# The spike gate of the first attention: a sigmoid by a power on GpSimd and a reciprocal on VectorE, in place of a ScalarE tangent

## The chip, the cores and the metric

The kernel runs on one core of a Trainium2 chip. The metric is device time in microseconds (us), the median of several runs. A core has five engines with a queue of instructions each, worked off in order: TensorE (PE, matmuls), VectorE (DVE), ScalarE (ACT, tabulated functions), GpSimd (POOL) and SyncE (SP, which here only issues DMAs). They wait for each other through semaphores.

## The reference

Two layers of the same form run over an input `x` of 4 batches x 1024 tokens x 128 channels:

```python
xn = _layernorm(x)
x  = x + attention0(xn) * silu(spiking_ffn(xn))
xn = _layernorm(x)
x  = x + attention1(xn) * silu(coupling_net(xn))
```

Both attentions have 16 heads of 8 channels. The change touches only the `silu` of the first layer. Its argument is the mean of five spikes:

```python
h = jnp.square(jax.nn.relu(xn @ W_fc.T)); y = h @ W_proj.T
mem_new = BETA * mem + y - reset * THRESHOLD       # 5 steps
spk = spike_fn(mem_new - THRESHOLD)                # 0 or 1
return jnp.sum(spks, axis=0) / NUM_STEPS           # n / 5, n = 0..5
```

So the gate is (n/5) * sigmoid(n/5), where n is a whole number from 0 to 5.

## The kernel before

The program has a prologue (norms, projections, transposes), the first attention, the coupling stage (the second layer's feed-forward net, which overlaps the end of the first layer) and the second attention.

The first attention is one long loop over 256 steps `t`: 4 batches of `PER` = 64 steps. A step takes four heads, one tile of 128 keys and 512 queries. For it PE computes scores (L1199, four matmuls, two "units" of 128x1024), ACT takes the exponential of each unit (L1001, two instructions per step), and PE multiplies the result with the values (L1214) into the accumulator `o_ps`. The queues are written out by hand. Three PSUM slots hold units of scores (`SLOTS` = 3), four buffers hold exponentials (`RING` = 4), and the product runs two steps behind the scores (`LAG` = 2). PE and DVE are written in pairs of steps; a batch has 32 pairs, and "pair r" below is the r-th pair of its batch.

Everything else of layer one is slipped into this loop as "side pieces". In each pair PE does at most one (`side_fills` gives the pair for each: the feed-forward `fc` at 5 to 8 and 14 to 17, `y` at 10 to 13 and 19 to 22, the output projection `mix` of the batch's first half at 27, the next layer's `q`, `k`, `v1`, `norm` of the batch before at 18, 23, 24 and 28 to 31). A piece lands in one PSUM bank, `side`. DVE must empty it (`evacuate`) before PE may start the next piece: `pe.wait_ge(side_in, n)` stands at the start of each, and PE's scores and products are queued behind it. Four times in a batch (`end`, pairs 9, 17, 25 and 1 of the next) DVE also transposes `o_ps` out (L1061), and PE's next product waits for that (`o_free`).

The gate belongs to halves `hf` of 512 tokens, tiles of 128x512. In DVE's queue `spike_op` makes n in `y` by 13 instructions from pair 14 (half 0) and pair 23 (half 1) on, two a pair. Then ACT computes tanh(n/10) into `th` (L1006; in the trace `th` has the name `ext`) at steps 42 and 62, and DVE multiplies (1 + tanh) by n (L1091, `gate`) at pair 22, and for half 1 at pair 1 of the next batch (pair 0 after the last). Since (n/5) * sigmoid(n/5) = (n/10) * (1 + tanh(n/10)), the factor `GATE_SCALE` = 1/10 is multiplied into the output weights. `update` on POOL then multiplies the projected attention by the gate (L1013) and adds it to `x` (L1016). POOL also squares the hidden units (L1027) and the `q` and `k` rows of the next layer (`norm_squares`, L1035). The half-norms (`half_norm_op`, small 128x4 instructions of L256 to L264) and `normed_half` (L839) follow on DVE.

After the last batch, `middle` takes over on every engine. Its DVE part waits for all gates (`gated`) before the last update (L1574, L1577, L1578).

Of the kernel before, what the change touches and what calls it, by code (L numbers as in the profile page):

```python
# [20 lines left out]
ALU = mybir.AluOpType  # L21
# [27 lines left out]
BETA = 0.9  # L49
MASK = -1.0e30  # L50
CYCLES = 3
GATE_SCALE = 0.5 / STEPS
ROOT_GUESS = 0x5F3759DF


# [756 lines left out]
def half_norm_tiles(sb):  # L812

    work = {name: sb(name, [P, HT]) for name in ("var", "fix", "root", "rstd")}
    work.update(stats=sb("stats", [P, HT, 6]), moments=sb("moments", [P, HT, 2]))
    return work
# [71 lines left out]
def first_attention(nc, a, s, ctx, room):  # L888
# [38 lines left out]
    th = [s["ext"][1][:, HALF * hf:HALF * hf + HALF].rearrange("p (t c) -> p t c", c=C) for hf in range(2)]  # L927
    square = [early_th1[1][:, HALF * hf:HALF * hf + HALF].bitcast(BF16).rearrange("p (z t) -> p z t", z=2) for hf in range(2)]
    work = half_norm_tiles(sb)

    scores, o_ps, side = room["scores"], room["o_ps"], room["side"]
    side_tiles = side[:, :].rearrange("p (t c) -> p t c", c=C)
# [4 lines left out]
    side_ps, side_in, hid_rdy = sem("side_ps"), sem("side_in"), sem("hid_rdy")  # L937
    xs0_rdy, skip_rdy, spiked, th_rdy, gated = (sem(x) for x in ("xs0_rdy", "skip_rdy", "spiked", "th_rdy", "gated"))
    scaled, updated, ln1, xs1_rdy, scaled_w = (sem(x) for x in ("scaled", "updated", "ln1", "xs1_rdy", "scaled_w"))
    sq_rdy = sem("sq_rdy")  # L940
    stored = [s[f"stored1{hf}"] for hf in range(2)]

    def tiles(b, hf):
        return slice(BT * b + HT * hf, BT * b + HT * hf + HT)
# [48 lines left out]
    def act_part(act):  # L993
        for t in range(S):
            b, gp, qh, gs, kt = place(t)
            if t >= RING:
                act.wait_ge(pv_done, t - RING + 1)
            for pair in range(2):
                unit = 2 * t + pair
                act.wait_ge(scored, unit + 1)  # L1000
                nc.scalar.activation(probs[t % RING][:, 2 * pair:2 * pair + 2, :], scores[unit % SLOTS][:, :, :],  # L1001
                                     ACT.Exp).then_inc(expd, 1)
            for hf, at in ((0, 42), (1, 62)):
                if t % PER == at:
                    act.wait_ge(spiked, SPIKE_OPS * (2 * b + hf + 1))
                    nc.scalar.activation(th[hf][:, :, :], s["y"][:, tiles(b, hf), :], ACT.Tanh,  # L1006
                                         scale=GATE_SCALE).then_inc(th_rdy, 1)

    def pool_part(pool):
        def update(b, hf):  # L1010
            pool.wait_ge(side_in, fill_index("mix", b, hf) + 1)
            pool.wait_ge(gated, 2 * b + hf + 1)
            pool.tensor_tensor(mix[hf][:, :, :], mix[hf][:, :, :], s["y"][:, tiles(b, hf), :], ALU.mult).then_inc(scaled, 1)  # L1013
            pool.wait_ge(scaled, 2 * b + hf + 1)
            x = s["x"][:, tiles(b, hf), :]
            pool.tensor_tensor(x, x, mix[hf][:, :, :], ALU.add).then_inc(updated, 1)  # L1016

        def skips(b):
            for hf in range(2):
                pool.wait_ge(xs0_rdy, 2 * b + hf + 1)  # L1020
                skip = s["xn"][:, tiles(b, hf), :]
                pool.tensor_tensor(skip, skip, s["bo"][:, 0:1, :].broadcast_to([P, HT, C]), ALU.add).then_inc(skip_rdy, 1)

        def squares(b, hf):
            for f in range(FC):
                pool.wait_ge(side_in, fill_index("fc", b, (hf, f)) + 1)
                pool.tensor_tensor(hidden[f], hidden[f], hidden[f], ALU.mult).then_inc(hid_rdy, 1)  # L1027

        def norm_squares(b, hf):
            for z in range(2):  # L1030
                pool.wait_ge(side_in, fill_index("qk"[z], b, hf) + 1)
                if b > 0:
                    pool.wait_ge(side_in, fill_index("norm", b - 1, hf) + 1)
                high = parts[hf][:, z, 0, :].bitcast(F32)
                pool.tensor_tensor(square[hf][:, z, :], high, high, ALU.mult).then_inc(sq_rdy, 1)  # L1035

        for b in range(B):
            if b > 0:
                update(b - 1, 1)
                skips(b)  # L1040
            squares(b, 0)
            if b == 0:
                pool.wait_ge(scaled_w, 1)
                skips(b)
            squares(b, 1)
            if b > 0:
                norm_squares(b - 1, 0)
            update(b, 0)
            if b > 0:
                norm_squares(b - 1, 1)  # L1050

    def dve_part(dve):
        ends, spike, norm1 = Chain(dve, end_link), Chain(dve, spiked), Chain(dve, ln1)

        def end(e):
            t = turn[e % 2]
# [31 lines left out]
        def gate(b, hf):  # L1088
            y = s["y"][:, tiles(b, hf), :]
            dve.wait_ge(th_rdy, 2 * b + hf + 1)  # L1090
            nc.vector.scalar_tensor_tensor(y, th[hf][:, :, :], 1.0, y, ALU.add, ALU.mult).then_inc(gated, 1)  # L1091

        def extra(b, r):
            if b == 0 and r == 9:
# [3 lines left out]
            if b == 0 and r == 13:  # L1098
# [2 lines left out]
                nc.vector.tensor_scalar_mul(s["bo"][:, 1, :], s["bo"][:, 1, :], 0.5)  # L1101
                nc.vector.tensor_scalar_mul(s["w1"][:, 0, :], s["w1"][:, 0, :], SCALE)
                nc.vector.tensor_scalar_mul(s["b_col1"][:, 0:1], s["b_col1"][:, 0:1], SCALE).then_inc(scaled_w, 1)
            if b > 0 and r == (0 if b == B else 1):
                gate(b - 1, 1)
            if b == 1 and r == 3:
                room["constants"](dve)
            if b < B:
# [6 lines left out]
                for k in range(SPIKE_OPS):  # L1115
                    for hf, at in ((0, 14), (1, 23)):
                        if r == at + k // 2:
                            spike_op(b, hf, k)
                if r == 22:
                    gate(b, 0)  # L1120
            for hf, at, own in ((1, 6, b - 1), (0, 29, b)):
                if 0 <= own < B and not (own == B - 1 and hf == 1):
# [1099 lines left out]
```

## Time and profile before

| | |
|---|---|
| median of 3 runs | 897.27 us (896.77 to 897.57) |
| profiled execution, first to last instruction | 894.0 us, so 3.3 us lie outside it, seen against the median |
| first attention (55.9 to 534.6 us) | 478.7 us |
| busy there | ACT 476.8, PE 454.5, DVE 241.0, POOL 84.2 us |
| coupling stage (534.6 to 602) | 67.4 us: PE 60.8, DVE 58.4, ACT 47.0 us |
| second attention (602 to 894) | 292.0 us |

The trace lists each instruction with its start, duration, engine, line, and output and input tiles. In brackets stands the idle time of its engine just before it, and what released it. Two matmul or ScalarE instructions in a row overlap in part, so the step from start to start is the cost of one in a full queue, and it is shorter than the duration. A share of busy time tells little here: what counts is which engine waits, in which pair, for whom.

### The profile page before, as it was taken

Reading aid. Unit: us, or ns where it says so; the run is one execution under the profiler, and the core shown is the slowest. Engines: PE = TensorE matmul, PEld = TensorE weight load, DVE = VectorE, ACT = ScalarE, POOL = GpSimd, SP = SyncE. Lnnn points to the kernel's source line nnn. Section 1 sums busy time; section 2 is a strip of 40 time slices with the busy share of each in tenths; the row PEclk is TensorE's granted clock in tenths of the full one; section 3 lists DMA queues with packets and bytes.
Section 4 is the critical chain, followed back from the end, with each engine's and each line's share of the span. In section 5 each row is a group of like instructions: output and inputs, shape, how many; then the busy total and the mean of one; then the engine's idle time right before and its main releaser. Section 6 shows DMA issues by size and latency. Waiting matters only on the chain.

```text
span 894.0 us, 22254 instructions
## 1 busy us (share of the span) xinstructions
PE 781.4 (87%) x9422; PEld 304.8 (34%) x9422; DVE 398.4 (45%) x862; ACT 832.1 (93%) x929; POOL 217.4 (24%) x260
## 2 busy tenths in 40 slices
PE   4849999899999999998999999978888888887876
PEld 2412434234343433433343333223333332332322
DVE  7821164454647553576327577994211021121122
ACT  7759999999999999999999996778999999999896
POOL 2201120121212041111303023103342443334343
PEclk9969999999999999999999999998999999999999
DMA  7882020110210301203000016000202202112000
GB/s 185 280 289 44 3 76 3 34 44 2 77 49 1 124 2 32 70 25 123 2 3 25 25 58 206 23 25 1 76 3 88 79 11 88 38 52 88 12 3 25
DMA packets 31950, 53.47 MB, mean 60 GB/s; under 512 B 5481, under 2 KB 16361, under 8 KB 31849
## 3 DMA queue, kind: packets, MB, share of 16 engines
q1 hardware_dynamic: 31848, 52.01, 18.7%
q8 instruction: 76, 1.25, 0.6%
q14 instruction: 26, 0.21, 0.1%
HBM read 31.29 MB, written 20.71 MB: 58 GB/s over the span
## 4 chain that ended last, share of the span: by engine, by line
PE 70%; ACT 18%; issue 3%; DVE 3%; ACTq 0%; DVEq 0%
PE c_ps L1214 25%; PE c_ps L1199 13%; ACT c_ring L1883 11%; PE c_ps L2071 10%; PE c_ps L112 10%; PE c_ps L2028 7%; ACT c_ring L1001 5%; PE c_ps L1619 2%; DVE early L1564 1%; PE c_ps L1634 1%; PE c_ps L1626 1%; ACT xs L1890 1%; ACT c_ring L1422 1%; DVE y L1567 1%; ACT ext L1006 0%
## 5 line engine op out<-in xcount | busy, mean ns | idle before, releaser
L1001 ACT ACTIVATE c_ring<-c_ps 128x1024 f32<-128x1024 f32 x512 | 473.7, 1034 | 9.5 <-PE c_ps L1199 9.2
L1883 ACT ACTIVATE c_ring<-c_ps 128x1024 f32<-128x1024 f32 x288 | 269.5, 1049 | 10.5 <-PE c_ps L2028 4.8
L1214 PE MATMUL c_ps<-c_ring,vt 128*18 128x256 f32 (+1 forms) x3072 | 271.3, 456 | 0.0
L1199 PE MATMUL c_ps<-q_st,k_st 32*128 32x512 f32 x1024 | 131.1, 500 | 28.8 <-ACT c_ring L1001 23.3
L2071 PE MATMUL c_ps<-c_ring,vt 128*18 128x256 f32 (+3 forms) x1856 | 154.0, 440 | 0.8
L1908 POOL TENSOR_SCALAR_AFFINE_SELECT c_ring<-c_ring 128x512 f32<-128x512 f32 x128 | 85.8, 690 | 191.7 <-ACT c_ring L1883 191.7
L2028 PE MATMUL c_ps<-q_st,k_st 32*128 32x512 f32 (+3 forms) x768 | 78.2, 422 | 51.3 <-ACT c_ring L1883 50.7
L1214 PEld LDWEIGHTS c_ps<-c_ring,vt 128*18 128x18 f32 x3072 | 65.2, 97 | 143.2 <-issue 103.0
L1199 PEld LDWEIGHTS c_ps<-q_st,k_st 32*128 32x128 f32 x1024 | 50.6, 183 | 144.7 <-ACT c_ring L1001 135.4
L1027 POOL TENSOR_TENSOR early<-early 128x512 f32<-128x512 f32 x32 | 38.4, 1201 | 177.4 <-DVE early L1138 177.4
L2028 PEld LDWEIGHTS c_ps<-q_st,k_st 32*128 32x128 f32 x768 | 36.9, 184 | 113.0 <-ACT c_ring L1883 103.1
L1942 DVE STREAM_TRANSPOSE ext<-c_ps 128x512 f32<-128x512 f32 x15 | 10.8, 717 | 135.5 <-PE c_ps L2071 135.5
L2071 PEld LDWEIGHTS c_ps<-c_ring,vt 128*18 128x18 f32 x1856 | 40.7, 97 | 70.3 <-issue 51.4
L1138 DVE TENSOR_SCALAR early<-c_ps 128x512 f32<-128x512 f32 x32 | 22.1, 690 | 67.2 <-PE c_ps L112 67.2
L1142 DVE TENSOR_SCALAR y<-c_ps,rho 128x128 f32<-128x128 f32 x32 | 9.0, 344 | 92.6 <-PE c_ps L112 92.6
L1013 POOL TENSOR_TENSOR early<-early,y 128x512 f32<-128x512 f32 x7 | 10.6, 1513 | 144.5 <-DVE early L1153 144.5
L1422 ACT ACTIVATE c_ring<-c_ps,cn_b 128x512 f32<-128x512 f32 (+1 forms) x30 | 25.1, 858 | 16.6 <-PE c_ps L1619 11.3
L1035 POOL TENSOR_TENSOR c_th<-parts 128x512 bf16<-128x512 f32 x12 | 15.1, 1256 | 82.7 <-DVE parts L1170 82.7
L112 PE MATMUL c_ps<-proj_t,early 128*32 128x128 f32 x1024 | 33.8, 273 | 0.0
L112 PE MATMUL c_ps<-y,fc_t 128*32 128x512 f32 x256 | 33.3, 592 | 0.0
L112 PEld LDWEIGHTS c_ps<-proj_t,early 128*32 128x32 f32 x1024 | 29.3, 110 | 5.9
L1084 DVE SCALAR_TENSOR_TENSOR c_th<-ext,c_th 128x512 f32<-128x512 f32 x24 | 25.5, 1061 | 0.7
(238 smaller groups left out, 727.4 us busy)
## 6 DMA issues: line engine op xcount, KB each, us to landing
q_st<-q_hl SPq DMA_DIRECT2D x48, 256.0 KB
k_st<-k_hl SPq DMA_DIRECT2D x48, 256.0 KB
q_hl<-parts SPq DMA_DIRECT2D x12, 512.0 KB, 4.4
k_hl<-parts SPq DMA_DIRECT2D x12, 512.0 KB, 4.7
q_hl<-early SPq DMA_DIRECT2D x4, 512.0 KB, 4.8
k_hl<-early SPq DMA_DIRECT2D x4, 512.0 KB, 5.2
out_dram<-x SPq DMA_DIRECT2D x7, 256.0 KB, 4.1
x<-in_L_attn_x_dram SPq DMA_DIRECT2D x3, 512.0 KB, 5.7
```

The costliest lines, as they stand in the source:

```text
L112: ins = nc.tensor.matmul(out[c:c + COLUMN, :], weight[:, c:c + COLUMN], rows, start=start, stop=stop, tile_position=(0, c))
L1001: nc.scalar.activation(probs[t % RING][:, 2 * pair:2 * pair + 2, :], scores[unit % SLOTS][:, :, :], ACT.Exp).then_inc(expd, 1)
L1027: pool.tensor_tensor(hidden[f], hidden[f], hidden[f], ALU.mult).then_inc(hid_rdy, 1)
L1084: ins = nc.vector.scalar_tensor_tensor(y if step == STEPS - 1 else count[:, :, :], m1, 1.0, count[:, :, :], ALU.is_gt, ALU.add)
L1138: ins = nc.vector.tensor_scalar_max(hidden[hf[1]], side[:, :], 0.0)
L1199: ins = nc.tensor.matmul(scores[(2 * t + i // 2) % SLOTS][:, i % 2, :], k_st[part, g, kt * P:(kt + 1) * P], q_st[part, g, qh * HALF:(qh + ...
L1214: ins = nc.tensor.matmul(o_ps[32 * h:32 * h + 2 * W9, c0:c1], vt[b % 2][:, kt, gp, h, W9 * gs:W9 * gs + 2 * W9], probs[t % RING][:, h, c0: ...
L1422: nc.scalar.activation(out, source, ACT.Gelu, bias=bias[:, 0:1]).then_inc(squashed[z], 1)
L1883: nc.scalar.activation(probs[t % RING][:, 2 * pair:2 * pair + 2, :], scores[unit % SLOTS][:, :, :], ACT.Exp).then_inc(expd, 1)
L1908: ins = pool.affine_select(out=part, in_=part, compare_op=ALU.is_ge, fill=0.0, base=0, pattern=[[0, G], [1, P]], channel_multiplier=-1)
L2028: ins = nc.tensor.matmul(banks[i][:, at:at + w], k_st[part, 2 * gp + gs, kt * P:(kt + 1) * P], q_st[part, 2 * gp + gs, qh * HALF + q0:qh * ...
L2071: ins = nc.tensor.matmul(o_ps[32 * h:32 * h + 2 * W9, q0:q0 + w], vt[b % 2][:, kt, gp, h, W9 * gs:W9 * gs + 2 * W9], probs[t % RING][:, h, ...
```

## The change

The gate's sigmoid becomes 1 / (1 + exp(-n/5)). The power `DECAY ** n` = exp(-n/5) is one POOL instruction per half (`powers`), with the constant base broadcast from a new tile `decay`. DVE's `gate` now has three dependent instructions: add 1, reciprocal, and the product with n. `GATE_SCALE` becomes 1/5. ACT's eight tangents are gone. In POOL's queue the power of half 0 comes behind the two squares of `norm_squares(b - 1, 0)`, that of half 1 behind `norm_squares(b - 1, 1)`. The gates stand later in DVE's queue: at pair 27 in place of 22, at pair 3 in place of 1, and after the last batch at pair 1 in place of 0, which puts it behind the last `end`.

```diff
-GATE_SCALE = 0.5 / STEPS
+GATE_SCALE = 1.0 / STEPS
+DECAY = float(np.exp(-GATE_SCALE))
...
-            for hf, at in ((0, 42), (1, 62)):
-                if t % PER == at:
-                    act.wait_ge(spiked, SPIKE_OPS * (2 * b + hf + 1))
-                    nc.scalar.activation(th[hf][:, :, :], s["y"][:, tiles(b, hf), :], ACT.Tanh,
-                                         scale=GATE_SCALE).then_inc(th_rdy, 1)
...
+        def powers(b, hf):
+            pool.wait_ge(spiked, SPIKE_OPS * (2 * b + hf + 1))
+            pool.tensor_tensor(th[hf][:, :, :], decay[:, :, 0:1].broadcast_to([P, HT, C]), s["y"][:, tiles(b, hf), :],
+                               ALU.pow).then_inc(th_rdy, 1)
...
+        pool.memset(decay[:, :, :], DECAY).then_inc(decay_rdy, 1)
+        pool.wait_ge(decay_rdy, 1)
...
             if b > 0:
                 norm_squares(b - 1, 0)
+            powers(b, 0)
             update(b, 0)
             if b > 0:
                 norm_squares(b - 1, 1)
+            powers(b, 1)
...
-            nc.vector.scalar_tensor_tensor(y, th[hf][:, :, :], 1.0, y, ALU.add, ALU.mult).then_inc(gated, 1)
+            below.after(nc.vector.tensor_scalar(th[hf][:, :, :], th[hf][:, :, :], 1.0, None, ALU.add))
+            below.after(nc.vector.reciprocal(th[hf][:, :, :], th[hf][:, :, :]))
+            nc.vector.tensor_tensor(y, y, th[hf][:, :, :], ALU.mult).then_inc(gated, 1)
...
-            if b > 0 and r == (0 if b == B else 1):
+            if b > 0 and r == (1 if b == B else 3):
                 gate(b - 1, 1)
...
-                if r == 22:
+                if r == 27:
                     gate(b, 0)
```

How the queues stand afterwards. First DVE in the last batch, around pairs 22 to 29. Of the program before: L1142 is the `y` evacuation at pair 22, L1091 the gate, L1153 the `mix` evacuation at pair 27, L1174 the `norm` evacuation at pair 28, L1169 and L1170 that of `q` at 29.

```order
L1142 TENSOR_SCALAR y<-c_ps,rho 128x128 x4
L1091 SCALAR_TENSOR_TENSOR y<-ext,y 128x512
L1169 TENSOR_SCALAR parts<-c_ps,b_col 128x512
L1170 SCALAR_TENSOR_TENSOR parts<-c_ps,b_col,parts 128x512
...
L1153 TENSOR_TENSOR early<-c_ps,xn 128x512
L1082 SCALAR_TENSOR_TENSOR ext<-ext 128x512
L1084 SCALAR_TENSOR_TENSOR c_th<-ext,c_th 128x512
L1174 TENSOR_REDUCE norms<-c_ps 64x1
```

The same stretch of the changed program, where these lines are L1151, L1178, L1179, L1162, L1089, L1091 and L1183:

```order
L1151 TENSOR_SCALAR y<-c_ps,rho 128x128 x4
L1178 TENSOR_SCALAR parts<-c_ps,b_col 128x512
L1179 SCALAR_TENSOR_TENSOR parts<-c_ps,b_col,parts 128x512
...
L1162 TENSOR_TENSOR early<-c_ps,xn 128x512
L1089 SCALAR_TENSOR_TENSOR ext<-ext 128x512
L1091 SCALAR_TENSOR_TENSOR c_th<-ext,c_th 128x512
L1098 TENSOR_SCALAR ext<-ext 128x512
L1099 RECIPROCAL ext<-ext 128x512
L1100 TENSOR_TENSOR y<-y,ext 128x512
L1183 TENSOR_REDUCE norms<-c_ps 64x1
```

The gate, now three instructions, moved from the front of this stretch to a place directly ahead of the `norm` evacuation.

Then POOL in the last batch, from the squares of the hidden units to the coupling stage (L1406, squares of the last half). Before:

```order
L1027 TENSOR_TENSOR early<-early 128x512 x8
L1035 TENSOR_TENSOR c_th<-parts 128x512 x2
L1013 TENSOR_TENSOR early<-early,y 128x512
L1016 TENSOR_TENSOR x<-x,early 128x512
L1035 TENSOR_TENSOR c_th<-parts 128x512 x2
L1406 TENSOR_TENSOR ext<-parts 128x512 x2
```

And in the changed program, where L1025 are the hidden squares, L1038 the row squares, L1029 the power, L1011 and L1014 the update:

```order
L1025 TENSOR_TENSOR early<-early 128x512 x8
L1038 TENSOR_TENSOR c_th<-parts 128x512 x2
L1029 TENSOR_TENSOR ext<-a_decay,y 128x512
L1011 TENSOR_TENSOR early<-early,y 128x512
L1014 TENSOR_TENSOR x<-x,early 128x512
L1038 TENSOR_TENSOR c_th<-parts 128x512 x2
L1029 TENSOR_TENSOR ext<-a_decay,y 128x512
L1415 TENSOR_TENSOR ext<-parts 128x512 x2
```

Each power stands behind a pair of row squares; the first is ahead of the update, the second ahead of whatever POOL does next.

## Rows read from the trace of the kernel before

**Rows 1.** Groups by line: line engine op tiles xcount | busy us, mean ns | idle before.
```profile
L1001 ACT ACTIVATE c_ring<-c_ps 128x1024 f32<-128x1024 f32 x512 | 473.7, 1034 | 9.5 <-PE c_ps L1199 9.2 <-issue 0.2
L1199 PE MATMUL c_ps<-q_st,k_st 32*128 32x512 f32 x1024 | 131.1, 500 | 28.8 <-ACT c_ring L1001 23.3 <-DVE c_ps L1177 4.6
L1006 ACT ACTIVATE ext<-y 128x512 f32<-128x512 f32 x8 | 5.1, 637 | 0.0
```

**Rows 2.** Busy time by engine (PE, PEld, DVE, ACT, POOL) in the first attention.
```profile
55.90:534.60 478.70, 454.54 (x6096) 176.13 (x6096) 241.04 (x514) 476.83 (x520) 84.22 (x66) 0.99 0.15 46
```

**Rows 3.** Timeline, ACT: start us, us, engine line op tiles xcount [idle before].
```profile
137.28 0.63 ACT L1006 ACTIVATE ext<-y 128x512 f32<-128x512 f32 x1
137.79 36.88 ACT L1001 ACTIVATE c_ring<-c_ps 128x1024 f32<-128x1024 f32 x40
```

**Rows 4.** Timeline, PE weight loads, last batch: waits for ACT in one pair.
```profile
502.12 0.19 PEld L1199 LDWEIGHTS c_ps<-q_st,k_st 32*128 32x128 f32 x4 [0.84 <-ACT c_ring L1001]
505.84 0.19 PEld L1199 LDWEIGHTS c_ps<-q_st,k_st 32*128 32x128 f32 x4 [0.20 <-ACT c_ring L1001]
506.73 0.12 PEld L1214 LDWEIGHTS c_ps<-c_ring,vt 128*18 128x18 f32 x4 [0.31 <-ACT c_ring L1001]
```

**Rows 5.** Timeline, POOL and DVE side by side, 119 to 126 us.
```profile
119.14 1.42 POOL L1027 TENSOR_TENSOR early<-early 128x512 f32<-128x512 f32 x1 [2.29 <-DVE early L1138]
119.70 1.41 DVE L1082 SCALAR_TENSOR_TENSOR ext<-ext 128x512 f32<-128x512 f32 x1
...
125.46 0.69 DVE L1082 SCALAR_TENSOR_TENSOR ext<-ext 128x512 f32<-128x512 f32 x1
```

**Rows 6.** Timeline, POOL and DVE side by side, 530 us.
```profile
530.02 1.04 POOL L1035 TENSOR_TENSOR c_th<-parts 128x512 bf16<-128x512 f32 x1 [2.67 <-DVE parts L1170]
...
530.04 1.03 DVE L264 SCALAR_TENSOR_TENSOR a_root<-a_fix,a_root 128x4 f32<-128x4 f32 x1
```

**Rows 7.** Groups by line and form, DVE: reciprocals of three sizes, and an add-like scalar instruction.
```profile
L138 DVE RECIPROCAL a_recip<-early 128x32 f32<-128x32 f32 x16 | 5.6, 353 | 0.5
L138 DVE RECIPROCAL a_recip<-ext 128x16 f32<-128x16 f32 x2 | 0.5, 252 | 0.1
L1078 DVE TENSOR_SCALAR c_th<-y 128x512 f32<-128x512 f32 x8 | 3.3, 417 | 0.0
```

**Rows 8.** Timeline, POOL: products of 128x512 with one and with two input tiles.
```profile
78.42 1.04 POOL L1027 TENSOR_TENSOR early<-early 128x512 f32<-128x512 f32 x1 [39.73 <-DVE early L1138]
193.75 1.31 POOL L1013 TENSOR_TENSOR early<-early,y 128x512 f32<-128x512 f32 x1 [30.23 <-DVE early L1153]
```

**Rows 9.** Timeline, last batch, pairs 24 and 25: POOL, DVE and PE.
```profile
503.88 1.15 POOL L1035 TENSOR_TENSOR c_th<-parts 128x512 bf16<-128x512 f32 x1 [17.55 <-DVE parts L1170]
504.17 1.41 DVE L1080 SCALAR_TENSOR_TENSOR ext<-y 128x512 f32<-128x512 f32 x1
...
506.59 0.68 DVE L1082 SCALAR_TENSOR_TENSOR ext<-y,ext 128x512 f32<-128x512 f32 x1
...
508.83 0.72 DVE L1061 STREAM_TRANSPOSE early<-c_ps 128x512 f32<-128x512 f32 x1 [0.83 <-PE c_ps L1214]
...
509.90 1.49 PE L1214 MATMUL c_ps<-c_ring,vt 128*18 128x512 f32 x16
```

**Rows 10.** Timeline, DVE, last batch, pairs 27 to 29.
```profile
516.99 0.69 DVE L1153 TENSOR_TENSOR early<-c_ps,xn 128x512 f32<-128x512 f32 x1 [1.78 <-PE c_ps L112]
...
524.31 0.75 DVE L1169 TENSOR_SCALAR parts<-c_ps,b_col 128x512 fp32r<-128x512 f32 x1 [1.93 <-PE c_ps L112]
```

**Rows 11.** Timeline, last batch, pair 31 and after: DVE and PE weight loads.
```profile
531.11 0.16 DVE L261 SCALAR_TENSOR_TENSOR a_fix<-a_root 128x4 f32<-128x4 f32 x1
...
532.18 0.68 DVE L1172 TENSOR_TENSOR xn<-c_ps,bv 128x512 f32<-128x512 f32 x1
...
533.55 0.10 PEld L1249 LDWEIGHTS c_ps<-c_th,head_of 128*32 128x32 bf16 x2
```

**Rows 12.** Timeline, DVE, start of the coupling stage.
```profile
539.61 0.69 DVE L1574 TENSOR_TENSOR early<-c_ps,xn 128x512 f32<-128x512 f32 x1 [1.11 <-PE c_ps L1688]
...
552.36 0.68 DVE L1541 TENSOR_REDUCE norms<-c_ps 64x1 f32<-64x512 f32 x1 [2.56 <-PE c_ps L1675]
```

**Rows 13.** Timeline, DVE, batch 0 after half 0's spikes, and batch 1's first pairs.
```profile
140.97 1.13 DVE L1142 TENSOR_SCALAR y<-c_ps,rho 128x128 f32<-128x128 f32 x4 [11.91 <-PE c_ps L112]
...
181.05 0.72 DVE L1061 STREAM_TRANSPOSE early<-c_ps 128x512 f32<-128x512 f32 x1 [10.80 <-PE c_ps L1214]
```

More of the change, by code:

```diff
@@ L929, in first_attention @@
     work = half_norm_tiles(sb)
+    decay = sb("decay", [P, HT, 1])
     scores, o_ps, side = room["scores"], room["o_ps"], room["side"]
@@ L939, in first_attention @@
     scaled, updated, ln1, xs1_rdy, scaled_w = (sem(x) for x in ("scaled", "updated", "ln1", "xs1_rdy", "scaled_w"))
-    sq_rdy = sem("sq_rdy")
+    sq_rdy, decay_rdy = sem("sq_rdy"), sem("decay_rdy")
+    denominator = sem("denominator")
     stored = [s[f"stored1{hf}"] for hf in range(2)]
@@ L1050, in pool_part @@
                 norm_squares(b - 1, 1)
+            powers(b, 1)
     def dve_part(dve):
-        ends, spike, norm1 = Chain(dve, end_link), Chain(dve, spiked), Chain(dve, ln1)
+        ends, spike, norm1, below = (Chain(dve, x) for x in (end_link, spiked, ln1, denominator))
         def end(e):
```

## The prediction

> **What bounds the kernel now.** I read the groups by line first, then the busy time by stage, then the timeline of each engine around the gates. In the first attention ACT is busy 476.8 of 478.7 us [rows 2]. Its 512 exponentials waited only 9.5 us in all, nearly all of it before the first [rows 1]. So ACT is full from the loop's start to its end, and a tangent in its queue costs its whole step: 137.28 to 137.79, 0.51 us [rows 3]. But the margins of the others are thin. PE waits for ACT only for 0.20 to 0.84 us ahead of a step's scores, the less the larger the side piece, and 0.31 us within the products [rows 4]. When PE comes later than that, ACT runs dry within a few exponentials. PE in turn waits for DVE wherever `side` or `o_ps` must be emptied. So I asked at each place where the change adds something how late DVE gets, and whether PE notices.
>
> **What is taken away.** Eight tangents at 0.51 to 0.52 us: -4.2 us, if nothing else gives way.
>
> **The reciprocal.** The trace has none of 128x512. Those of L138 take 353 ns for 32 elements a row and 252 ns for 16 [rows 7]: 6.3 ns per element. Carried on to 512 that is 0.353 + 480 x 0.0063 = 3.4 us. With the addition (as L1078, 0.42 us [rows 7]) and the product (0.69 us [rows 5]) the gate holds DVE for 4.5 us; before it was 0.7. Ends: if the slope belonged only to small strided rows, a 128x512 instruction of DVE takes 0.69 us [rows 5], and the gate 1.8; above, I allow 4.5 us for the reciprocal, a third more than the slope. I take 3.4, since both rows are of the very operation.
>
> The Trainium skill (VectorE: DVE Perf Modes, "First, the fixed hardware budget") says that a reciprocal is an iterated divide with a repeat count of 8. At the 0.96 GHz of the same page's specifications that is an estimated 4.3 us for 512 elements; the rows show 6 rather than 8 such cycles per element, and they decide. By the page the forecast would be some 3 us higher.
>
> **The power.** No row shows one. From below, it does at least what a POOL product of two tiles does, 1.31 us [rows 8]. From above I build it out of passes: a logarithm, a product and an exponential, each function a polynomial of several terms, make at most some 20 operations; each costs no more than a whole product pass of 1.04 us [rows 8], 21 us together. The ends are a factor 16 apart, and no row is near. I take their geometric mean, 5.2 us (five product passes), and call it X. The duration is not the whole cost, because of the following.
>
> **What a POOL instruction does to DVE.** L1082 takes 0.69 us alone. It took 1.41 us when it started at 119.70 inside the POOL product of 119.14 to 120.56, and ended 0.55 us behind it: it made no progress in between [rows 5]. A DVE instruction of 128x4, too, took 1.03 us and ended with the POOL instruction beside it [rows 6]. So DVE instructions with two SBUF inputs stand still while POOL works on SBUF. If that holds for the power, everything in DVE's queue waits up to X.
>
> For products of 1 us the rows show this; that a long, computing instruction holds the port to its end they don't. The Trainium skill (SBUF — State Buffer, "Who interferes with whom") has it so: the pair of ports is an exclusive lock that the first instruction keeps to its end. By that rule the sum is the one below; if the port were free while the power computes, it would be about 4 us.
>
> **Place A, the power of half 0** (batches 1 to 3). It is behind the second row square, which ends at 505.03; the DVE instruction already waiting goes first and ends at 505.58 [rows 9]. So the power runs 505.6 to 510.8. L1082, due at 506.59, and the spike instruction behind it then end at 512.2, and the `o_ps` transpose at 512.95 in place of 509.55. PE's first product of the next step, which started at 509.90 [rows 9], waits for it: 3.05 us late, of which 0.3 are PE's slack [rows 4]. Stall 2.8 us, three times: 8.3. In batch 0 no row squares stand ahead; the power starts with DVE's 11.9 us of idle time [rows 13] and is free.
>
> **Place B, the gate at pair 27** (batches 1 to 3). From L1153 to the `q` evacuation DVE has 1.93 us of idle time [rows 10]. The gate brings 4.5. The `norm` evacuation behind it and then `q` and `k` are late by 2.6 us; less 0.5 of PE's slack (the middle of 0.20 to 0.84 [rows 4]) that is 2.1, three times: 6.3. In addition the POOL update starts about 5.7 us later and blocks DVE among the following evacuations rather than before: DVE's and POOL's queues go into pair 31 about 1.8 us behind ACT (0.5 of the slack used, 1.3 for one POOL instruction).
>
> **Place C, the power of half 1** (batches 1 and 2). It starts behind the last row square, 531.1, and holds DVE's small root instructions until 536.3; six of them (531.11 to 532.18) and L1172 (0.68) follow [rows 11], so `v1` is emptied at 538.05 in place of 532.86. PE's `norm` piece, which began at 533.55 [rows 11], waits: 4.5 us, with the lag 6.3. Up to two and a half exponentials of 0.92 us (36.88/40 [rows 3]) are in stock, 2.3 us. Stall 4.0, twice: 8.0. After batch 0 DVE is idle for 10.8 us [rows 13]: free. The gate at pair 3 there falls into idle time.
>
> **The end.** In the last batch nothing covers place C: PE's last products, the last `end` and the coupling stage's PE queue all come 6.3 us later. The gate now stands behind that `end`, so L1574, which had 1.11 us to spare, is 3.4 us late against PE; 2.56 us of idle time at 552.36 [rows 12] take most of that back. I put down 0.5 (between 0 and 0.9). The second attention is unchanged.
>
> **Sum.** -4.2 + 8.3 + 6.3 + 8.0 + 6.3 + 0.5 = +25.2 us. The profiled span is 894.0, so 919.2; with the 3.3 us by which the median of the runs lies above it, 922.5.
>
> With X the sum moves by 6 us per us (three places A, two C, the end), once X is over some 3.5. Below, A is free up to 2.4 and C up to 1.2. X = 3.5 gives +15, X = 8 gives +42, X = 10 gives +54, X = 12 gives +66, X = 21 gives +120.
>
> **Rivals.**
> 1. *The power is cheap, or leaves DVE's port alone.* With X = 1.31: -4.2, A 0, B 6.3, C 0.2, end 1.31 + 1.1 = 2.4, and 0.5: +5.2, 902.5. With a free port and X under 8 about the same (+4, 901). For it: no row shows a computing instruction hold the port. Against: the power is no single arithmetic step.
> 2. *A long power*, 8.5 us and more: +45 to +120, 942 to 1017. For it: a general power with its special cases may be longer than five passes. Against: only my way of counting.
> 3. *Faster: the reciprocal streams.* At 0.69 us the gate is 1.8 us, less than the 1.93 of idle time at B, so B costs nothing and no lag is left. With X = 1.31 the end costs some 1.5 us: -4.2 + 1.5 + 0.3 = -2.4, 894.9. It decides at X = 2.3 with such a reciprocal, and with one of 2 us only if X is under 1.5. Against it stand the two sizes of [rows 7].
> 4. *Nothing to be measured*: these cancel by chance, X about 2.3 with a short reciprocal.
> That ACT isn't relieved at all I rule out: the tangents are gone from its queue, and none is left to load or run.
>
> **How the numbers follow.** Forecast (port held, X 3.5 to 8.5): 0.42, with its own range of 910 to 943. Rival 1: 0.26 (X up to 3.5 with the port held, to 912, included). Rival 2: 0.20. Rival 3: 0.07. Rival 4: 0.05. The range leaves out rival 3, rival 4 in part, and powers over 12 us (about 0.1): 899 to 964. A difference of under 0.2% (1.8 us) can't be told from none here: faster 0.08, same 0.05, slower 0.87.
>
> **What would show it.** POOL's rows of the power give X; the row of the 128x512 reciprocal should read 3.4 us. With the port held, a DVE instruction behind each power has a duration of nearly X, and ACT has idle gaps that it doesn't have now: about 2.8 us at pair 25, some three of together 2 at pairs 28 to 30, 4 us at pair 0 of the next batch, none in batch 0. If the port is free, DVE's rows beside the power keep 0.69 us. The forecast is wrong if ACT shows no gaps at pairs 28 to 30 though the reciprocal takes over 3 us, or if the coupling stage takes up or gives back more than 1 us.

## The result, and the profile after

The changed kernel takes 1438.08 us (median of 4 runs, 1436.89 to 1438.62) against 897.02 us for the kernel before: 1.6038 times as long, 95% interval 1.6016 to 1.606. The forecast of 922.5 us, and its range up to 964, were far too low. The direction was right, the reason only in part.

The groups by line of the kernel after (columns as in [rows 1]) name the place at once.

```profile
L1004 ACT ACTIVATE c_ring<-c_ps 128x1024 f32<-128x1024 f32 x512 | 474.7, 1032 | 476.8 <-PE c_ps L1208 476.2
L1029 POOL TENSOR_TENSOR ext<-a_decay,y 128x512 f32<-128x512 f32 x8 | 656.8, 82097 | 4.9 <-DVE y L1091 4.9
...
L1098 DVE TENSOR_SCALAR ext<-ext 128x512 f32<-128x512 f32 x8 | 4.2, 531 | 539.8 <-POOL ext L1029 539.8
...
L1099 DVE RECIPROCAL ext<-ext 128x512 f32<-128x512 f32 x8 | 26.8, 3353 | 0.3
```

One power (L1029) takes 82.1 us. DVE's addition (L1098), the first instruction of each gate, waits 539.8 us for it in all. The exponentials (L1004) do the same work as before, 474.7 against 473.7 us, but stand idle for 476.8 us instead of 9.5 [rows 1]. The reciprocal takes 3.35 us.

The slices of the page (busy tenths in 40 slices, 36 us each) show the same as a picture.

```profile
PE   5699804039910801993061099405007888888887
...
DVE  8314213044500502451060135305008911121112
ACT  7699913029920800993062099503005799999997
POOL 2015989961499798139979822997992133333333
PEclk9799956569965855997576599757658999999999
```

POOL is full through most of the first attention (up to slice 28) while ACT, which was full in [rows 2], works in bursts. Where PE is at 0, the clock falls too.

How one engine's wait stops the others is read from ACT's timeline (start us, us, instructions, idle time before them), one line per power. The first:

```profile
177.73 5.67 ACT L1004 ACTIVATE c_ring<-c_ps 128x1024 f32<-128x1024 f32 x6
228.60 3.95 ACT L1004 ACTIVATE c_ring<-c_ps 128x1024 f32<-128x1024 f32 x4 [45.21 <-PE c_ps L1208]
```

The next two, and one that is no longer in the first attention:

```profile
312.41 1.94 ACT L1004 ACTIVATE c_ring<-c_ps 128x1024 f32<-128x1024 f32 x2 [70.67 <-PE c_ps L1208]
...
1083.78 0.26 ACT L1474 ACTIVATE n_gu<-c_ps,cn_gb 64x2 f32<-64x2 f32 x1 [73.41 <-PE c_ps L1669]
```

Five more gaps lie between the last two: 70.44 us before 472.62, 731.09 and 988.52, 66.7 us before 570.20 and 828.79. The seven gaps up to 988.52 are 460.6 us together; the eighth is in the coupling stage. What ACT is said to wait for is PE; what PE waits for stands in the list of waits (engine, line, for what: us in total, times, longest).

```profile
DVE ext L1098 <- POOL ext L1029: 539.8, 8, 74.8
...
PE c_ps L113 <- DVE norms L1183: 207.6, 3, 69.2
...
PE c_ps L113 <- DVE early L1162: 200.3, 3, 69.4
...
PE c_ps L1669 <- DVE n_mean L1560: 74.4, 1, 74.4
...
PE c_ps L1223 <- issue: 43.7, 1, 43.7
```

So the chain is power, addition, everything queued behind it on DVE (`norms`, `early`, `n_mean`), PE's next piece of work, and with it the scores that ACT needs. Behind six of the powers PE stands at a side piece whose bank DVE has not emptied. Behind the eighth it waits for the norm of the coupling stage. The first gap goes another way: no side piece is due there, and the trace names no releaser for PE's product at 225.01 ("issue"). It starts 0.1 us after DVE's transpose of `o_ps` has ended, for which that product waits in the program (`o_free`):

```profile
224.20 0.71 DVE L1068 STREAM_TRANSPOSE early<-c_ps 128x512 f32<-128x512 f32 x1
```

The account of the profiled execution, 1436.3 against 894.0 us, +542.3. The first attention ends with ACT's table load at 998.95, before at 534.62: +464.3. Of that +467.3 are idle time before L1004 (476.8 - 9.5), +1.0 its busy time, and -4.2 the eight tangents as forecast: +464.1. The coupling stage runs from there to the next table load, 141.5 us against 64.4: +77.1, of which 73.4 is the eighth gap. The remaining 0.9 us lies behind it.

### The profile page after: what moved, and what is told of

Read it like the earlier page. It is cut to its first block, busy times and chain, and to the rows that moved or that the text cites. A ratio compares the mean times of both kernels' runs of the same rounds, so it can differ in the third digit from the quotient of the medians.

```text
span 1436.3 us, 22272 instructions
## 1 busy us (share of the span) xinstructions
PE 799.6 (56%) x9422; PEld 306.6 (21%) x9422; DVE 433.1 (30%) x878; ACT 830.4 (58%) x921; POOL 872.3 (61%) x269
## 4 chain that ended last, share of the span: by engine, by line
POOL 46%; PE 33%; ACT 8%; DVE 7%; issue 2%; ACTq 0%; DVEq 0%
POOL ext L1029 46%; PE c_ps L1223 10%; PE c_ps L2080 6%; ACT c_ring L1892 6%; PE c_ps L113 5%; PE c_ps L1208 5%; PE c_ps L2037 5%; DVE ext L1099 2%; PE c_ps L1628 1%; DVE early L1573 1%; ACT c_ring L1004 1%; POOL c_th L1038 0%; PE c_ps L1643 0%; DVE ext L1087 0%; DVE parts L1179 0%
## 5 line engine op out<-in xcount | busy, mean ns | idle before, releaser
L1004 ACT ACTIVATE c_ring<-c_ps 128x1024 f32<-128x1024 f32 x512 | 474.7, 1032 | 476.8 <-PE c_ps L1208 476.2
L1029 POOL TENSOR_TENSOR ext<-a_decay,y 128x512 f32<-128x512 f32 x8 | 656.8, 82097 | 4.9 <-DVE y L1091 4.9
L1223 PE MATMUL c_ps<-c_ring,vt 128*18 128x256 f32 (+1 forms) x3072 | 278.5, 466 | 43.7 <-issue 43.7
L1892 ACT ACTIVATE c_ring<-c_ps 128x1024 f32<-128x1024 f32 x288 | 269.6, 1048 | 11.2 <-PE c_ps L2043 5.2
L1098 DVE TENSOR_SCALAR ext<-ext 128x512 f32<-128x512 f32 x8 | 4.2, 531 | 539.8 <-POOL ext L1029 539.8
L1208 PE MATMUL c_ps<-q_st,k_st 32*128 32x512 f32 x1024 | 133.4, 509 | 27.1 <-ACT c_ring L1004 20.8
L1025 POOL TENSOR_TENSOR early<-early 128x512 f32<-128x512 f32 x32 | 38.4, 1199 | 162.6 <-DVE early L1147 162.6
L113 PE MATMUL c_ps<-y,w 128*32 128x512 f32 x96 | 15.2, 709 | 207.6 <-DVE norms L1183 207.6
L1038 POOL TENSOR_TENSOR c_th<-parts 128x512 bf16<-128x512 f32 x12 | 15.1, 1256 | 73.3 <-DVE parts L1179 73.3
L113 PEld LDWEIGHTS c_ps<-y,fc_t 128*32 128x32 f32 x256 | 8.2, 113 | 207.0 <-DVE early L1162 201.7
L113 PEld LDWEIGHTS c_ps<-y,w 128*32 128x32 f32 x96 | 2.9, 117 | 210.7 <-DVE norms L1183 209.1
```

Of the source, the lines that this page charges most:

```text
L113: ins = nc.tensor.matmul(out[c:c + COLUMN, :], weight[:, c:c + COLUMN], rows, start=start, stop=stop, tile_position=(0, c))
L1029: pool.tensor_tensor(th[hf][:, :, :], decay[:, :, 0:1].broadcast_to([P, HT, C]), s["y"][:, tiles(b, hf), :], ALU.pow).then_inc(th_rdy, 1)
L1208: ins = nc.tensor.matmul(scores[(2 * t + i // 2) % SLOTS][:, i % 2, :], k_st[part, g, kt * P:(kt + 1) * P], q_st[part, g, qh * HALF:(qh + ...
L1223: ins = nc.tensor.matmul(o_ps[32 * h:32 * h + 2 * W9, c0:c1], vt[b % 2][:, kt, gp, h, W9 * gs:W9 * gs + 2 * W9], probs[t % RING][:, h, c0: ...
```

## The experiments

All but the one marked are compared with the kernel before on the same chip. Its median was 896.16 us for the first three, 896.21 for the four from "The product, with half 0's gate at pair 26" on, and 896.43 for the last. A difference in us is the ratio with its interval, applied to that median. Where the power is replaced or cut down, the values are not the reference's; these kernels only price it.

**A product in place of the power.** Everything else of the change stays, so this prices the change with a short POOL instruction: it takes 1.04 to 1.48 us.

```
-                               ALU.pow).then_inc(th_rdy, 1)
+                               ALU.mult).then_inc(th_rdy, 1)
```

> The changed kernel with a POOL product in place of the power, same tiles, same place in the queue (so the gate's value is not the reference's). Theory 1 (the power's own length, 82 us, makes the loss; everything else in my sum is right): the sum at X = 1.31 us stands, -4.2 for the tangents, +6.3 at the gates of pair 27, +2.4 at the end, +0.2 +0.5: +5.2 us, 902; ACT shows idle gaps of together about 2 us at pairs 28 to 30 of batches 1 to 3. Rival (the longer gate is hidden, only the power cost anything): -4.2 + at most 1, so 893 to 894, no ACT gaps.

Measured: 900.91 us, ratio 1.0056 (1.0043 to 1.0068), so +5.0 us. ACT's timeline at pairs 28 to 30 of batch 1:

```profile
287.81 3.79 ACT L1004 ACTIVATE c_ring<-c_ps 128x1024 f32<-128x1024 f32 x4 [0.79 <-PE c_ps L1208]
292.66 3.79 ACT L1004 ACTIVATE c_ring<-c_ps 128x1024 f32<-128x1024 f32 x4 [1.05 <-PE c_ps L1208]
297.03 110.98 ACT L1004 ACTIVATE c_ring<-c_ps 128x1024 f32<-128x1024 f32 x120 [0.58 <-PE c_ps L1208]
```

Three gaps, 2.4 us together; batches 2 and 3 show 2.2 and 2.4. That is place B of the prediction. By the medians, 1438.08 - 900.91, the power's length is worth 537 us of the change's cost, all but five.

The sum agrees better than its terms do. Place B is 7.0 us in place of 6.3. The end, put down at 2.4 + 0.5 us, shows no gap of its own: the coupling stage takes 65.2 us here and 64.6 with the narrow power below, against 64.4 before. (This profiled execution took 903.1 us, 2.2 above the median; it has one more gap, 1.28 us at 70.84, that the narrow power's does not show.)

**The product, and no reciprocal.** The gate loses its reciprocal, which changes the values and leaves 1.1 us of work on DVE.

```
-            below.after(nc.vector.reciprocal(th[hf][:, :, :], th[hf][:, :, :]))
```

> As the product kernel, and the reciprocal left out as well, so that the gate is an addition and a product, 1.1 us of DVE. Theory 1 (place B is DVE's hold of 4.5 us against 1.93 us of idle time): the gaps at pairs 28 to 30 go, the sum is -4.2 plus some 1.5 to 2 at the end: about -2.4, 894.6. Rival (the gate's place at pair 27 costs, not its length): as the product kernel within 1 us.

Measured: 893.44 us, ratio 0.9975 (0.9964 to 0.9986), so -2.2 us. The gaps at pairs 28 to 30 are gone:

```profile
279.03 12.97 ACT L1004 ACTIVATE c_ring<-c_ps 128x1024 f32<-128x1024 f32 x14
292.21 8.36 ACT L1004 ACTIVATE c_ring<-c_ps 128x1024 f32<-128x1024 f32 x9 [0.21 <-issue]
```

The reciprocal alone makes the difference of 7.5 us between this kernel and the product kernel. Rival 3 had the sum for this case, -2.4; here too the terms differ. The loop, from ACT's second group of exponentials to its table load, is 3.2 us shorter than before rather than 4.2, and the coupling stage is 64.6 us, so that of the 1.8 us at the end 0.2 are seen.

**A narrow power.** A power on 32 of each row's 512 elements: long enough to tell whether DVE's port is held, short enough to end before every gate (L1102, the addition, waits 0.0 us in its trace). The other elements hold what a product wrote in batch 0.

```
-            pool.tensor_tensor(th[hf][:, :, :], ..., ALU.pow).then_inc(th_rdy, 1)
+            pool.tensor_tensor(th[hf][:, :, 0:8], ..., ALU.pow).then_inc(th_rdy, 1)
```

(`th[hf]` holds 4 tiles of 128, so 0:8 of each is 32 elements a row. The product of batch 0 stands in lines that are not shown.)

> The changed kernel with the power taken on 32 of each row's 512 elements (8 of 128 columns; the rest of the tile is filled once by a product and then left as it is, so the gate's value is not the reference's). If 82 us is a price per element, 160 ns each, the power now takes 5.1 us, the length that I had forecast. Theory 1 (the power leaves DVE's port free, so that only the wait in the gate costs, and 5.1 us end before the gate is due): +4 us, 901, DVE's instructions beside it at 0.69 us. Rival (port held, as in the forecast): +25 us, 922, with a DVE instruction of up to 5 us behind each power.

Measured: 901.32 us, ratio 1.0065 (1.005 to 1.0079), so +5.8 us, the product kernel's time within the intervals. POOL's power and the DVE instructions beside it, in batch 3 at place A:

```profile
506.19 5.87 POOL L1033 TENSOR_TENSOR ext<-a_decay,y 128x32 f32<-128x32 f32 x1
```

```profile
507.17 0.69 DVE L1185 TENSOR_TENSOR xn<-c_ps,bv 128x512 f32<-128x512 f32 x1 [0.40 <-PE c_ps L113]
507.78 0.68 DVE L1093 SCALAR_TENSOR_TENSOR ext<-y,ext 128x512 f32<-128x512 f32 x1
508.50 0.69 DVE L1095 SCALAR_TENSOR_TENSOR c_th<-ext,c_th 128x512 f32<-128x512 f32 x1
510.01 0.72 DVE L1072 STREAM_TRANSPOSE early<-c_ps 128x512 f32<-128x512 f32 x1 [0.82 <-PE c_ps L1227]
```

This power has almost exactly the X of my forecast (5.6 us on average, 5.2 taken). By the forecast the kernel should have cost +25 us. It does not, because the DVE instruction with two SBUF inputs at 507.78 takes its usual 0.68 us in the middle of the power. So the port is not held through the power: the second assumption of the forecast falls, independently of the power's length.

**The power by itself** (one execution; its total time is not compared). Eight POOL instructions one after the other, appended to the kernel before at the end of its second attention.

```
+ go(pool.tensor_tensor(res[:, 0:128], base[:, 0:128], bent[:, 0:128], ALU.pow))   # 0.81873 ^ 3
+ go(pool.tensor_tensor(res[:, 0:32], ...))  and  0:4,  and 16 partitions
+ go(... five ...)   go(... half ...)   go(... ALU.mult)   go(bent ^ half)
```

> The kernel before with POOL instructions appended to the end of POOL's queue, on tiles that nothing else uses: powers of 128x128, 128x32, 128x4 and 16x128, of 128x128 with exponents 3, 5 and 0.5 and with base 3, and one product of 128x128. Theory 1 (a price per element of a row, whatever the values, partitions side by side): 20.5, 5.1 and 0.7 us for the widths, 20.5 us for 16 partitions too, and the same for every exponent. Rival a (a large fixed part, such as code that is loaded): the narrow ones far above 160 ns per element. Rival b (the price depends on the values): exponents 0.5 and 5 differ from 3 by over 10%. The time of the whole kernel is longer by the appended work and is not compared.

Their rows, in that order, from POOL's timeline:

```profile
893.48 20.80 POOL L1949 TENSOR_TENSOR bench<-bench 128x128 f32<-128x128 f32 x1
914.36 5.43 POOL L1950 TENSOR_TENSOR bench<-bench 128x32 f32<-128x32 f32 x1
919.87 1.01 POOL L1951 TENSOR_TENSOR bench<-bench 128x4 f32<-128x4 f32 x1
920.95 20.77 POOL L1952 TENSOR_TENSOR bench<-bench 16x128 f32<-16x128 f32 x1
941.80 20.78 POOL L1953 TENSOR_TENSOR bench<-bench 128x128 f32<-128x128 f32 x1
962.66 20.77 POOL L1954 TENSOR_TENSOR bench<-bench 128x128 f32<-128x128 f32 x1
983.51 0.45 POOL L1955 TENSOR_TENSOR bench<-bench 128x128 f32<-128x128 f32 x1
984.04 20.77 POOL L1956 TENSOR_TENSOR bench<-bench 128x128 f32<-128x128 f32 x1
```

From 32 to 128 elements a row: (20.80 - 5.43)/96 = 0.160 us per element, and 0.3 us that is fixed. 512 x 0.160 = 82 us, which is what the changed kernel shows. Sixteen partitions cost as much as 128, and exponents 3, 5 and 0.5 and bases 0.82 and 3 cost the same. A product of 128x128 takes 0.45 us, 1/46 of the power. So the price is one of each element of a row, and neither the other values tried nor fewer partitions lower it.

**The product, with half 0's gate at pair 26.** The forecast put place B down to the meeting of the gate with the side pieces of pairs 27 to 29. If so, one pair earlier is enough.

```
-                if r == 27:
+                if r == 26:
```

> The product kernel (a POOL product in place of the power) with the gate of half 0 at pair 26 in place of 27. Pair 26 has no side piece, so more of DVE's idle time lies behind the gate before PE needs the next bank. Theory (place B is a matter of which pair takes DVE's 4.5 us): the gaps of together 2.1 to 2.4 us in batches 1 to 3 shrink to under 0.5, some 5 us less than the product kernel, so 895 to 896, about the time before. Rival (DVE's hold costs the same wherever it stands): as the product kernel, 901.

Measured: 894.21 us, ratio 0.9978 (0.9967 to 0.999), so -2.0 us; 6.7 less than the product kernel. In its timeline ACT goes through pairs 26 to 31 with one gap of 0.20 us. So place B needs both the long gate and this position: either change by itself removes it. What the move would be worth behind an 82-us power was not run.

**The position alone.** The kernel before, tangents and all, with its gates at the changed kernel's places.

```
-            if b > 0 and r == (0 if b == B else 1):
+            if b > 0 and r == (1 if b == B else 3):
...
-                if r == 22:
+                if r == 27:
```

> The kernel before, tangents and one-instruction gate kept, with the gates at pairs 27, 3 and 1 in place of 22, 1 and 0. Theory (0.7 us of DVE at pair 27 fits into 1.93 us of idle time): within 0.5 us of before. Rival (a late gate delays the update of x and with it the squares, norms and the next layer's rows): 1 to 3 us slower.

Measured: 895.48 us, ratio 1.000 (0.9989 to 1.001). A gate of 0.7 us costs nothing in these places.

**A gate without tangent and power, two instructions.** `y` holds spike counts, whole numbers from 0 to 5. On these a quadratic fits the sigmoid to within 4.4 parts in 10,000, so that y times the gate is a cubic; its scale goes into the kernel's existing constant.

```
-                    nc.scalar.activation(th[hf][:, :, :], ..., ACT.Tanh, scale=GATE_SCALE).then_inc(th_rdy, 1)
...
-            nc.vector.scalar_tensor_tensor(y, th[hf][:, :, :], 1.0, y, ALU.add, ALU.mult).then_inc(gated, 1)
+            below.after(nc.vector.scalar_tensor_tensor(th[hf][:, :, :], y, -41.369491771299835, y, ALU.add, ALU.mult))
+            nc.vector.scalar_tensor_tensor(y, th[hf][:, :, :], -388.1519156907403, y, ALU.add, ALU.mult).then_inc(gated, 1)
```

The gates stay at the places of the kernel before, pairs 22, 1 and 0, and not at those of the change.

> The kernel before without tangents and without POOL: n takes only the values 0 to 5, so DVE evaluates the sigmoid as a quadratic in n, the gate as n times it: two instructions with two inputs each, (n + c) * n and then (that + d) * n, at the gate's old places; the factor goes into the output weights. Largest relative error of the gate 4e-4. Theory (ACT is full, a tangent costs its 0.52 us, and 0.7 us more of DVE at pairs 22, 1 and 0 lies in idle time): -4.2 + 0.3 at the last gate, 892 to 892.5. Rival (ACT was not the bound, PE is, the relief is lost): within 1 us of before.

Measured: 894.42 us, ratio 0.9977 (0.9963 to 0.999), so -2.1 us. It is faster than both kernels, by less than expected. In its timeline the exponentials run from 65.51 to the table load at 531.61, 466.1 us; before it was 65.30 to 534.62, 469.3. So 3.2 of the 4.2 us of tangents come out. It has two gaps of 0.2 us, where the kernel before has one; the second is:

```profile
529.65 1.94 ACT L1001 ACTIVATE c_ring<-c_ps 128x1024 f32<-128x1024 f32 x2 [0.21 <-issue]
```

The other 0.8 us is in the pace of the exponentials, which no row puts down to a cause. The kernels without tangents and without gaps at pairs 28 to 30 agree: their loops are 2.8 us (gate at pair 26) and 3.2 us (no reciprocal, two instructions, three instructions) shorter than before. The coupling stage then takes 64.8 us instead of 64.4.

**The same with three instructions.** A fit to within 2.4 parts in 100,000. The other constants change too; the added line is:

```
+            below.after(nc.vector.scalar_tensor_tensor(th[hf][:, :, :], th[hf][:, :, :], -446.7958912964597, y, ALU.add, ALU.mult))
```

> As the cubic gate with one instruction more (a cubic for the sigmoid, largest relative error 2.4e-5), so the gate holds DVE for 2.1 us. Theory: the third instruction costs nothing in the loop and up to 0.7 us at the last gate, which stands ahead of the last transpose: 892.3 to 893. Rival (DVE's margin is used up): 2 us and more over the cubic gate.

Measured: 894.15 us, ratio 0.998 (0.9965 to 0.9995), so -1.8 us. It can't be told from the two-instruction gate; its coupling stage is 0.7 us longer, 65.5 us. The last gate stands ahead of that stage on DVE and is one instruction longer; but two kernels with the same gates, the product's and the narrow power's, differ there by 0.5 us as well, so that this is not shown to be the reason.

**A quarter of the power.** 128 of each row's 512 elements, made as the narrow one. This asks whether the gap follows the power's length by a fixed amount.

```
+            pool.tensor_tensor(th[hf][:, :, 0:32], ..., ALU.pow).then_inc(th_rdy, 1)
```

> As the narrow power, but on 128 of each row's 512 elements: 21 us by the price per element (the gate's value is not the reference's). Theory (the power costs only by what it sticks out over the time from its start to its gate, some 12 to 15 us at seven places, 31 in batch 0's first half): no wait at the first gate, 4 to 10 us of idle ACT at each of the next six, about 12 us at the last gate, which the coupling stage takes over but for a few: together +50 to +58 us, 947 to 954. Rival (port held: also everything between is blocked): +110 us and more.

Measured: 961.07 us, ratio 1.0717 (1.0699 to 1.0735), so +64.3 us, above what I expected. The power (L1033) and the gate's addition (L1102), from the groups by line:

```profile
L1033 POOL TENSOR_TENSOR ext<-a_decay,y 128x128 f32<-128x128 f32 x8 | 167.2, 20897 | 0.2
...
L1102 DVE TENSOR_SCALAR ext<-ext 128x512 f32<-128x512 f32 x8 | 4.2, 530 | 57.4 <-POOL ext L1033 57.4
```

And ACT behind a gate of half 0 and one of half 1:

```profile
300.91 1.94 ACT L1004 ACTIVATE c_ring<-c_ps 128x1024 f32<-128x1024 f32 x2 [9.23 <-PE c_ps L1212]
303.78 5.64 ACT L1004 ACTIVATE c_ring<-c_ps 128x1024 f32<-128x1024 f32 x6 [0.93 <-PE c_ps L1212]
309.61 22.18 ACT L1004 ACTIVATE c_ring<-c_ps 128x1024 f32<-128x1024 f32 x24 [0.19 <-issue]
337.30 1.94 ACT L1004 ACTIVATE c_ring<-c_ps 128x1024 f32<-128x1024 f32 x2 [5.51 <-PE c_ps L1212]
340.68 79.71 ACT L1004 ACTIVATE c_ring<-c_ps 128x1024 f32<-128x1024 f32 x86 [1.44 <-PE c_ps L1212]
```

From batch 1 on, a power of half 0 takes 21.2 us here and leaves a gap of 9.2: 12 us are covered. In the changed kernel it takes 82.4 and leaves 70.4: again 12. For half 1 it is 20.7 - 5.5 = 15.2 here, and 81.9 - 66.7 = 15.2 there. So each gap is the power's length less a cover that the distance between power and gate sets. This holds for the five gaps of batches 1 to 3, and roughly in the coupling stage (20.7 - 11.8 = 8.9 us, and 81.9 - 73.4 = 8.5). The first power has a cover of 36.7 us in the changed kernel (81.95 - 45.21), and its quarter accordingly shows no gap. The second power fits less well: 20.7 - 5.9 = 14.8 us here, 81.9 - 70.7 = 11.2 there. In the changed kernel the spike instructions ahead of that power were themselves held up by the first gate, and DVE was at the next gate 11.8 us after the power's start; here it took 15.4. So the cover is not a constant of the place: an earlier stall can use it up.

What I had left out is the second, smaller gap behind each (0.93 and 1.44 above, 7.4 us over the six gates), and most of the coupling stage: 80.2 us, +15.8.

## Why the prediction was wrong

**The step that failed: the price of the power.** The forecast bounded it from above as "at most some 20 operations" of a product pass each, 21 us, and took the geometric mean with 1.31, 5.2 us. It is 82.1 us, some sixty to eighty product passes, and the 20.8 us of a mere quarter already reaches my upper end. The error is in the bound: I counted the arithmetic of a good polynomial and called the count a maximum, though no row showed a POOL instruction that computes a function. The range took over this false end. With no row near, the two ends were not measured bounds, and the middle between them was no estimate; the honest reading of "no row" would have left a chance for a power so long that the whole plan hangs on it.

**The second wrong step: the port.** From [rows 5] and [rows 6], where DVE stands still beside products of about 1 us, I concluded that a power would hold DVE's port to its end. Beside the 82-us power of 129.09 the DVE rows read:

```profile
145.37 0.69 DVE L1087 SCALAR_TENSOR_TENSOR ext<-y 128x512 f32<-128x512 f32 x1
...
148.64 0.68 DVE L1089 SCALAR_TENSOR_TENSOR ext<-y,ext 128x512 f32<-128x512 f32 x1
149.36 0.69 DVE L1091 SCALAR_TENSOR_TENSOR c_th<-ext,c_th 128x512 f32<-128x512 f32 x1
```

They run at their usual speed, and so do all 33 instructions of the spikes (two SBUF inputs, 128x512) that lie inside a power, 1.6 to 31.2 us after its start: 0.65 to 0.69 us. Further in, DVE has none to show. Only right at a power's start is one stretched. It is so with the powers of half 1 in batches 1 to 3 (479.77, 738.36, 995.71), each time to 0.96 us; the last:

```profile
995.80 0.96 DVE L262 SCALAR_TENSOR_TENSOR a_fix<-a_root 128x4 f32<-128x4 f32 x1
996.80 0.16 DVE L264 TENSOR_TENSOR a_fix<-a_fix,a_var 128x4 f32<-128x4 f32 x1
```

It ends 1.05 us into the power, 0.8 us later than its 0.16 would have it, and the next one is undisturbed. The same instruction behind the same power of 128 and of 32 elements a row (quarter and narrow power):

```profile
308.16 0.32 DVE L262 SCALAR_TENSOR_TENSOR a_fix<-a_root 128x4 f32<-128x4 f32 x1
...
535.35 0.16 DVE L262 SCALAR_TENSOR_TENSOR a_fix<-a_root 128x4 f32<-128x4 f32 x1
```

It ends 0.42 us into the quarter's power and is not stretched by the narrow one. 1.05 and 0.42 us are about what a POOL product of these widths takes (1.04 us for 512 elements, 0.45 for 128). So a power seems to stop DVE for one pass over its elements at its start, and then no more; the pass is inferred from these rows. The places A and C (8.3 and 8.0 us) and most of the end (6.3) therefore did not exist as described, and the sign named for them, no gaps in batch 0, failed too: the gaps behind its two powers are 45.2 and 70.7 us. The Trainium skill (SBUF — State Buffer, "Who interferes with whom") has an exclusive lock that lasts for the whole instruction. The products of this kernel agree; the power does not, and the measurement decides. For the same reason my "6 us per us of X" was the wrong slope with the wrong cause: with X = 82 it would give some 487 us, near the result by accident. Between the quarter and the whole power the span grows by 476.5 us for 61.2 us of length, 7.8 per us: all eight gates wait, the first one in part.

**What took their place.** The gate's own wait. The prediction knew the distance: it wrote that with a free port the change costs about 4 us as long as X is "under 8". Beyond that DVE, which works its queue in order, stands at L1098 until the power is done. Eight powers are 656.8 us, of which 539.8 are waited for; 117 us are hidden, 32 of them behind the first. There the power starts at 129.09, DVE reaches the gate at 160.99, and PE and ACT work on to 183. Rival 2, "a long power", had the right direction but the same bound of 21 us and the same held port, and so ended at 1017.

**A smaller miss: the tangents.** They were put down at -4.2 us. In the kernels where nothing else fills their place the loop is 2.8 to 3.2 us shorter. That the account of the first attention closes to 0.2 us with -4.2 does not test the term, beside 467 us of idle time.

**What was right.** The reciprocal, 3.4 us by the slope of [rows 7] and 3.35 measured; that is 6.5 ns an element at 128x512, close to the 6.3 ns of the slope. The Trainium skill (VectorE: DVE Perf Modes, "First, the fixed hardware budget") gives a repeat count of 8 and no time. The estimate of 4.3 us that the prediction made of it, 8 cycles per element, is refuted here. Place B, 2.1 us each time forecast, 2.2 to 2.4 measured in the product kernel, at the three pairs named; it goes away without the reciprocal, and with the gate one pair earlier. Rival 1's sum for a short power, +5.2, against +5.0; rival 3's for a short reciprocal, -2.4, against -2.2. That the moved gates by themselves cost nothing. The two sums are in part luck: place B came out 0.7 us higher than forecast, the relief by the tangents about 1 us smaller, and the end some 2 us smaller. So the model of place B held; one input, which no row supplied, was off by a factor of sixteen.

**What stays open.** The second gaps behind the quarter's gates were not tested by a run of their own; the clock below fits them. That the power stops DVE for one pass at its start rests on five rows at three widths. Where the missing 1 us of the tangents goes is not known. A gate placed 80 us behind its power was not tried: half 1's distance to the end of the stage does not allow it in the last batch, and the powers alone are 657 us of POOL in a first attention of 479, so by this sum POOL would be the bound wherever the gates stand.

## What to carry to other kernels

An operation that no row of the profile shows has no upper bound from arithmetic: run it once by itself, at two widths, before anything is planned around it. Here one run of eight instructions gives 0.160 us per element, and with it the 82 us that decide. Then compare its total on its engine with the stage it is to hide in, and remember that an engine that works its queue in order passes a wait on to all who need anything queued behind it, less only the distance between producer and consumer, which an earlier stall can shorten.

Where an instruction holds a shared port, look at the pair concerned: short products and a long function need not behave alike. And where a function's argument takes only a few whole values, a polynomial of two instructions can replace it (here with an error of up to 4.4 parts in 10,000).

## What the runs showed of the hardware

- The power on POOL costs 0.160 us per element of a row, whatever the partitions (16 or 128) and the values.
- It leaves DVE's two-input instructions at 0.69 us beside it from 1.6 us after its start on, while products of 1 us stop them (1.41 us, [rows 5]). At its start it stretched one from 0.16 to 0.96 us at 512 elements a row, to 0.32 at 128, and not at 32.
- TensorE's granted clock fell while PE stood idle, and the first work after the wait was slow. Two stretches of the kernel after, by engine as in [rows 2]:

```profile
241.00:311.00 70.00, 1.35 (x8) 0.20 (x8) 8.91 (x26) 0.74 (x1) 61.87 (x2) 0.51 0.00 0
345.00:400.00 55.00, 53.63 (x724) 20.69 (x714) 32.01 (x46) 55.00 (x60) 25.67 (x7) 1.00 0.15 51
```

The clock is 0.51 (the 1.2 GHz level) while PE waits, and 1.00 (2.4 GHz) in full work. PE's first group behind the wait, and the same one again 6 us later:

```profile
309.65 1.93 PE L113 MATMUL c_ps<-y,fc_t 128*32 128x512 f32 x8 [69.39 <-DVE early L1162]
...
315.44 1.04 PE L113 MATMUL c_ps<-y,fc_t 128*32 128x512 f32 x8
```

It takes nearly twice as long. The clock is still at the lower level two microseconds after PE's start, and the products of that stretch take 2.39 us where the same group takes 1.49 at 316.85:

```profile
311.60:313.50 1.90, 1.90 (x12) 0.54 (x16) 0.69 (x1) 1.09 (x2) 1.90 (x2) 0.50 0.00 0
...
312.24 2.39 PE L1223 MATMUL c_ps<-c_ring,vt 128*18 128x512 f32 x16
```

ACT's small gap of 0.81 us ahead of 315.16 lies in the same stretch, behind the one of 70.67. In the quarter's kernel it is the same: in the 2-us slices with its second gaps (302 to 304 and 338 to 340) the clock is 0.79 and 0.50, and PE's products ahead of them take 2.5 and 2.8 us. A slow PE behind each stall is thus a likely reason for the second gaps, though no run separates it from the rest.
